# Expert weights split piecewise during attention and kept in DRAM, routing in two halves of the graphs, stage memory laid out anew: a graph attention layer followed by a mixture of experts on one core

## What is computed

```python
def gnn(x, adj, Wq, Wk, Wv, bv, Wo, bo):              # x is layernormed first
    q, k, v = x @ Wq.T, x @ Wk.T, x @ Wv.T + bv       # split into 12 heads of 32
    a = einsum('bnhd,bmhd->bhnm', q, k) * 384 ** -0.5 + adj[:, None]
    a = softmax(where(all(a == 0, -1), -inf, a))      # a row of zeros gives zeros
    return einsum('bhnm,bmhd->bnhd', a, v) @ Wo.T + bo

def moe(x, router_w, router_b, w1, b1, w2, b2, ln_g, ln_b):   # x is layernormed first
    logits = x.mean(axis=1) @ router_w.T + router_b   # one choice for each graph
    top_v, top_i = top_k(logits, 2); gates = softmax(top_v)
    h = act[e](x @ w1[e] + b1[e])                     # act: gelu, silu, mish, gelu
    y = sum(gate[e] * (h @ w2[e] + b2[e])) + x        # w1: 384x768, w2: 768x384
    return layernorm(y) * ln_g + ln_b

x = x + gnn(layernorm(x), adj, ...)
x = x + moe(layernorm(x), ...)
```

## Time and profile before

| | |
|---|---|
| median of 3 runs | 1682.14 us (1681.82 to 1683.52) |
| profiled execution | 1679.88 us, span 1678.1 us |
| TensorE busy | 1598.1 us, 95% of the span |
| VectorE, ScalarE, GpSimd busy | 1191.3, 953.4 and 826.9 us (71%, 57% and 49%) |
| TensorE's share of the chain that ended last | 88% |
| mean granted TensorE clock | 0.982 |
| DMA | 159.32 MB, 95 GB/s over the span |

### The profile page before, as it was taken

How to read it: one execution, slowest core, us unless ns; L and a number is a source line. 1 busy time by engine, 2 the same in 40 slices (tenths; PEclk the granted TensorE clock), 3 DMA queues, 4 the chain that set the end, 5 groups by cost and what they waited for, 6 DMA issues and landing times.

```text
span 1678.1 us, 44889 instructions
## 1 busy us (share of the span) xinstructions
PE 1598.1 (95%) x12732; PEld 1531.1 (91%) x12733; DVE 1191.3 (71%) x3613; ACT 953.4 (57%) x2780; POOL 826.9 (49%) x1239
## 2 busy tenths in 40 slices
PE   6999999999999999837999999999999999999997
PEld 6899999999999999727999999999999999999997
DVE  4788888888888887776666665666776766567764
ACT  4888888888888888744332332332433423243332
POOL 2777777777777777760233333323333233323333
PEclk9999999999999999958999999999999999999999
DMA  7233333333333332550122222222222222221221
GB/s 242 67 116 114 120 121 121 116 116 121 121 121 121 121 119 97 178 216 20 62 72 70 70 70 70 70 70 70 70 70 70 70 70 70 70 70 62 79 64 36
DMA packets 81260, 159.32 MB, mean 95 GB/s; under 512 B 8672, under 2 KB 46560, under 8 KB 80992
## 3 DMA queue, kind: packets, MB, share of 16 engines
q1 hardware_dynamic: 81120, 157.58, 27.6%
HBM read 94.64 MB, written 62.91 MB: 94 GB/s over the span
## 4 chain that ended last, share of the span: by engine, by line
PE 88%; DVE 5%; ACT 2%; issue 2%; SPq 1%; POOL 1%; DMA 1%; DVEq 0%; POOLq 0%; ACTq 0%
PE bank L368 68%; PE bank L437 5%; PE bank L526 5%; PE bank L396 3%; PE bank L460 3%; PE bank L477 2%; PE bank L469 1%; PE bank L446 1%; DMA x_in<-in_x 1%; DVE half_t L1027 1%; DVE inverse L1034 1%; DVE inverse L1030 1%; ACT at_hi L688 1%; ACT inverse L721 1%; ACT prob L599 1%
## 5 line engine op out<-in xcount | busy, mean ns | idle before, releaser
L368 PE MATMUL bank<-w_hi,ut_in 128*128 x1536 | 423.2, 343 | 32.3 <-issue 27.9
L599 ACT ACTIVATE prob<-att,neg_max 128x128 f32<-128x128 f32 x768 | 297.4, 391 | 34.4 <-DVE neg_max L871 34.3
L368 PEld LDWEIGHTS bank<-w_hi,ut_in 128*128 128x128 f32 x1536 | 280.8, 189 | 37.0 <-issue 37.0
L987 DVE SCALAR_TENSOR_TENSOR at_lo<-bank,gate_col,at_hi 128x384 fp32r<-128x384 f32 x256 | 146.1, 613 | 185.2 <-ACT at_hi L688 185.2
L368 PE MATMUL bank<-w_hi,at_hi 128*128 x768 | 258.0, 336 | 5.6 <-DVE at_lo L987 5.6
L368 PE MATMUL bank<-w_lo,ut_in 128*128 x768 | 257.9, 336 | 0.0
L368 PE MATMUL bank<-w_hi,at_lo 128*128 x768 | 257.1, 335 | 0.0
L368 PE MATMUL bank<-w_lo,at_hi 128*128 x768 | 256.7, 334 | 0.0
L688 ACT ACTIVATE at_hi<-bank,gate_col 128x384 fp32r<-128x384 f32 x256 | 134.5, 576 | 202.9 <-PE bank L526 201.0
L845 POOL TENSOR_SCALAR rs_z<-mv_z 128x1 f32<-128x1 f32 x64 | 14.7, 229 | 473.8 <-DVE mv_z L1053 473.8
L712 ACT ACTIVATE hid<-hid 128x384 f32<-128x384 f32 x192 | 95.1, 527 | 268.9 <-DVE hid L999 268.9
(11 more groups left out here) (136 smaller groups left out, 3820.9 us busy)
## 6 DMA issues: line engine op xcount, KB each, us to landing
xu_scratch<-xu SPq DMA_DIRECT2D x64, 384.0 KB, 2.3
ut_scratch<-ut_out SPq DMA_DIRECT2D x64, 384.0 KB, 2.7
ut_in<-ut_scratch SPq DMA_DIRECT2D x64, 384.0 KB, 2.9
xz<-xu_scratch SPq DMA_DIRECT2D x64, 384.0 KB, 3.0
x_in<-in_x SPq DMA_DIRECT2D x32, 384.0 KB, 4.4
xu<-in_x SPq DMA_DIRECT2D x32, 384.0 KB, 3.5
out_dram<-xz SPq DMA_DIRECT2D x64, 192.0 KB, 1.9
w_lo<-in_L_ffn_w SPq DMA_DIRECT2D x8, 1152.0 KB, 9.8
```

What stands on the lines that cost most here:

```text
L368: last = nc.tensor.matmul(acc, lhs[c][a], rhs[c][b], start=start and n == 0, stop=stop and n == len(terms) - 1)
L599: nc.scalar.activation(prob[g][:, hh, :], att[g][:, head, :], ACT.Exp, bias=neg_max[g][:, head:head + 1], scale=-1.0, accum_out=row_sum[g] ...
L987: nc.vector.scalar_tensor_tensor(out=flat(at_lo[:, s * DC:(s + 1) * DC, :]), in0=at_ps[s][:, 0:HALF], scalar=gate_col[:, col, 1:2], in1=fl ...
```

## The change

The expert weights are split during attention, in 48 pieces of 128x384, one at each step from 4 to 51. ScalarE rounds the piece into one of three staging tiles, VectorE subtracts, SP stores. For w1 the `lo` half stays where it was loaded and only the `hi` half goes to DRAM; for w2 the raw piece is loaded into a staging tile, and both halves go to DRAM. At the end of attention SP loads the halves back (`load_early`, steps 54 and 62 to 66), each as soon as the attention tiles under it are free; so do b1, b2 and the first two expert inputs. The stage memory is laid out so that these addresses come free in this order. Routing is done for 32 graphs at a time: the first half in steps 36 to 44 of attention, the second inside the expert steps of graphs 0 and 1. The gates come from tanh instead of exp and a division. ScalarE and VectorE wait at the start of the expert stage for the stores of attention, as SP did; the layernorm weights and the third and fourth `xz` are loaded when the second half of routing is done.

The new engine parts, cut to their core:

```diff
+    ROUTED = B // 2
+    PIECES = E * FC          # 24
+    FIRST = 4
+    w1h_dram = nc.dram_tensor("w1h_scratch", (E, P, DC, F), F32, kind="Internal").ap()
+    w2_dram = nc.dram_tensor("w2_scratch", (2, E, P, FC, D), F32, kind="Internal").ap()
...
+        def piece(h):
+            return h - FIRST if 0 <= h - FIRST < 2 * PIECES else None
+        def piece_tiles(j):
+            if j < PIECES:
+                e, c, s = j // FC, j % FC // 2, j % 2
+                return w1_lo[:, e, c, s * HALF:(s + 1) * HALF], stage_hi[j % 3][:]
+            return stage_lo[j % 3][:], stage_hi[j % 3][:]
...
# SP
-                if h == B - 1:
-                    sp.wait_ge(s_mm, B)
-                    for e in range(E - 1):
-                        load_w2(e)
-                    sp.wait_ge(exp_done, HEADS * (B - 1))
-                    sp.wait_ge(fold_done, FOLDS * (B - 1))
-                    load_w2(E - 1)
+            def store_piece(j):
+                sp.wait_ge(piece_lo, j + 1)
+                if j < PIECES:
+                    e, c, s = j // FC, j % FC // 2, j % 2
+                    sp.dma_start(w1h_dram[e, :, c, s * HALF:(s + 1) * HALF], stage_hi[j % 3][:].bitcast(F32)).then_inc(hi_stored[j % 3], 16)
+                else:
+                    e, c = (j - PIECES) // FC, (j - PIECES) % FC
+                    sp.dma_start(w2_dram[1, e, :, c], stage_hi[j % 3][:].bitcast(F32)).then_inc(hi_stored[j % 3], 16)
+                    sp.dma_start(w2_dram[0, e, :, c], stage_lo[j % 3][:].bitcast(F32)).then_inc(lo_stored[j % 3], 16)
+            def load_early(h):
+                if h == FIRST + 2 * PIECES + 2:
+                    for p in range(3):
+                        sp.wait_ge(hi_stored[p], 16 * (2 * PIECES // 3))
+                        sp.wait_ge(lo_stored[p], 16 * (PIECES // 3))
+                    load_w1_hi(0)
+                if h == B - 2:
+                    sp.wait_ge(qk_mm, 2 * B)
+                    load_w1_hi(1)
+                    load_w1_hi(2)
+                    sp.wait_ge(v_mm, B)
+                    load_w1_hi(3)
+                    sp.dma_start(b1_wide[:]...).then_inc(wide_loaded, 16)
+                    sp.wait_ge(xn_done, B)
+                    sp.dma_start(b2_wide[:]...).then_inc(wide_loaded, 16)
+                    sp.wait_ge(xt_mm, B)
+                    sp.wait_ge(ut_stored[0], 16)
+                    load_ut(0, 0)
+                if h == B - 1:
+                    sp.wait_ge(s_mm, B)
+                    load_w2(0, 0)
+                    sp.wait_ge(exp_done, HEADS * (B - 1))
+                    sp.wait_ge(fold_done, FOLDS * (B - 1))
+                    load_w2(0, 1)
+                if h == B:
+                    sp.wait_ge(exp_done, HEADS * B)
+                    sp.wait_ge(fold_done, FOLDS * B)
+                    load_w2(0, 2)
+                if h == B + 1:
+                    sp.wait_ge(pt_mm, PTC * B)
+                    load_w2(0, 3)
+                    sp.wait_ge(o_mm, B)
+                    load_w2(1, 0)
+                    sp.wait_ge(ot_done, B)
+                    load_w2(1, 1)
+                    sp.wait_ge(v_done, B)
+                    sp.wait_ge(xbo_done, B)
+                    sp.wait_ge(ut_stored[1], 16)
+                    load_ut(1, 1)
+                if h == B + 2:
+                    sp.wait_ge(wo_mm, B)
+                    load_w2(1, 2)
+                    load_w2(1, 3)
             for h in STEPS:
...
+                if piece(h - 1) is not None:
+                    store_piece(piece(h - 1))
+                if piece(h + 1) is not None and piece(h + 1) >= PIECES:
+                    load_piece(piece(h + 1))
+                load_early(h)
                 n = h - 3
                 if has(n):
                     reached(sp, u_done, n + 1)
# TensorE
+            def logits(half):
+                graphs = slice(half * ROUTED, (half + 1) * ROUTED)
+                pe.wait_ge(pooled_done, (half + 1) * ROUTED)
+                pe.wait_ge(const_ready, 2)
+                reached(pe, routed, half)
+                for e in range(E):
+                    for c in range(DC):
+                        last = nc.tensor.matmul(bank[7][:, D + e * ROUTED:D + (e + 1) * ROUTED], rw_wide[:, c, e, :], pooled[:, graphs, c],
+                                                start=c == 0, stop=c == DC - 1)
+                last.then_inc(logit_mm, 1)
             for h in STEPS:
...
+                if h == ROUTED + 4:
+                    logits(0)
                 if has(h - 1):
                     attend(h - 1)
...
+            logits(1)
             pe.wait_ge(routed, 1)
+            pe.wait_ge(w1h_loaded, 16 * E)
+            pe.wait_ge(piece_lo, PIECES)
...
+                            pe.wait_ge(w2_loaded, 32 * E)   # before the first second_layer
# ScalarE
+                reached(act, hi_stored[j % 3], 16 * (j // 3))
+                nc.scalar.activation(rounded, raw_piece.bitcast(F32), ACT.Copy).then_inc(piece_hi, 1)
...
+                nc.scalar.activation(g_tmp[:, 1, :], g_tmp[:, 0, :], ACT.Tanh, scale=0.5).then_inc(tanh_gap, 1)
             for h in STEPS:
                 if has(h - 2):
                     round_o(h - 2)
+                if h == B:
+                    nc.scalar.preload_act_table(ACT.Gelu)
                 if has(h + 4):
                     round_x(h + 4)
+                if piece(h) is not None:
+                    round_piece(piece(h))
+                if h == ROUTED + 10:
+                    tanh_of_gap(0)
                 if has(h):
                     exps(h, (0, 1))
...
             act.wait_ge(routed, 1)
+            for g in range(2):
+                for p in range(2):
+                    act.wait_ge(xu_stored[p][g], 16 * (B // 4))
+                act.wait_ge(ut_stored[g], 16 * (B // 2))
# VectorE
                 if has(h - 3):
                     sum_nodes(h - 3)
+                if piece(h) is not None:
+                    rest_of_piece(piece(h))      # wait piece_hi; lo = raw - rounded
                 if has(h - 1):
                     divide(h - 1)
                 if has(h + 2):
                     take_v(h + 2)
                 if has(h):
                     greatest_part(h)
+                if h == ROUTED + 5:
+                    route_choice(0, 0)           # 9 chained instructions on [P, 32, 4] or [P, 32]
+                if h == ROUTED + 7:
+                    route_choice(0, 1)           # 7
+                if h == ROUTED + 12:
+                    route_gates(0)               # 6; the fourth waits for the tanh
+            dve.wait_ge(routed, 1)
+            for g in range(2):
+                for p in range(2):
+                    dve.wait_ge(xu_stored[p][g], 16 * (B // 4))
...
             def expert_step(b, m, lap):
...
                     if graph(b, 0):
                         activate_second(b, k, e)
+                    if isinstance(b, int) and b == 0:
+                        route_choice(1, k)
+                    if isinstance(b, int) and b == 1 and k == 0:
+                        route_gates(1)
```

More of the change, by code:

```diff
@@ L87, in gnn_moe_kernel @@
         bv_wide = sb("bv_wide", [P, D], F32, s1)
+        bo_wide = sb("bo_wide", [P, D], F32, s1)
+        q_t = [sb(f"q_t{p}", [P, DC, 2 * N], F32, s1) for p in range(2)]
+        k_t = [sb(f"k_t{p}", [P, DC, 2 * N], F32, s1) for p in range(2)]
         raw = ExitStack()
@@ L119, in gnn_moe_kernel @@
         shift2 = [sb(f"shift2{g}", [P, 1], F32, s1) for g in range(2)]
-        sb("gap", [P, 640], F32, s1)
+        adj_in = [sb(f"adj_in{p}", [P, 2, N], F32, s1) for p in range(2)]
+        sb("gap", [P, 1024], F32, s1)
         rw_t = sb("rw_t", [P, DC, E], F32, s1)
@@ new lines, in load_w1_hi, with load_w2, load_ut @@
+            def load_w1_hi(e):
+                sp.dma_start(w1_hi[:, e].bitcast(F32), w1h_dram[e]).then_inc(w1h_loaded, 16)
+            def load_w2(half, e):
+                sp.dma_start((w2_lo, w2_hi)[half][:, e].bitcast(F32), w2_dram[half, e]).then_inc(w2_loaded, 16)
+            def load_ut(b, m):
+                source = ut_dram[b] if isinstance(b, int) else ut_dram[bass.ds(b, 1)].rearrange("o p s c n -> (o p) s c n")
+                sp.dma_start(ut_in[m % 2][:].bitcast(F32), source).then_inc(ut_loaded[m % 2], 16)
@@ L503, in _ @@
                     transpose_x(h + 5)
-            pe.wait_ge(pooled_done, B)
-            pe.wait_ge(const_ready, 2)
-            for e in range(E):
-                for c in range(DC):
-                    last = nc.tensor.matmul(bank[4][:, e * B:(e + 1) * B], rw_wide[:, c, e, :], pooled[:, :, c],
-                                            start=c == 0, stop=c == DC - 1)
-            last.then_inc(logit_mm, 1)
-            pe.wait_ge(routed, 1)
+            logits(1)
+            pe.wait_ge(routed, 1)
+            pe.wait_ge(w1h_loaded, 16 * E)
+            pe.wait_ge(piece_lo, PIECES)
+            pe.wait_ge(pt_act, 2 * B)
+            pe.wait_ge(pt_vec, B)
+            pe.wait_ge(ot_done, B)
```

(23 more changed lines are left out.)

185 lines of the change are left out of this document (77 added, 108 removed).

## The result

The changed kernel takes **1690.68 us** (median of 5 runs, 1689.87 to 1694.05) against 1682.14 for the kernel before. The ratio is 1.0056, 95% interval 1.0045 to 1.0066: slower by about half a per cent. The prediction was 1674.2, with 0.82 on faster, and 1690.7 lies outside its range of 1661 to 1682. The profiled execution took 1692.06 us, with a span of 1690.3.

A forecast was written before the change was run, and what follows sets the result against it. TensorE was taken to bound steady attention and the experts, leaving about 33 us at the hand-over. Hand-over and tail -14.0 plus attention +6.1 gave -7.9 us: 1674.2 against the median 1682.14, range 1661 to 1682.

The forecast's parts named there:

- about 33 us lie open to this change; all else can only lose: Hand-over from attention to experts, 728.38 to 761.74 us: the only stretch where the change was held able to gain.
- rival A: The forecast itself: the DMA queue ends the hand-over; range 1669 to 1679 us, chance 0.60.
- D: Hand-over: the store wait grows until the expert stage starts as late as before; no change, 1682 us, chance 0.10.
- C: Attention: the pieces lengthen the steady step, up to 0.5 us each, 1698 us; chance 0.15 for some such cost.
- 48 pieces at 0: Steady attention: weight-split pieces, one a step, fit existing waits and slack and cost 0 us; upper bound 24.
- logits(0) at +2.6: Attention: the first half's logits, 12 fp32 products in 24 records, add 2.6 us on TensorE; bounds 1.3 and 5.1.
- Routing in attention at 3.5: VectorE's two choices and gates for the first half add 2.0, 1.3 and 0.2 us; bounds 0 and 8.1.
- The tail: End of attention: residual load queued behind 6.29 MB lands 5.9 us late, less 0.72 of wait, delaying everything after by 5.2.
- The queue ends the hand-over: Hand-over: attention's last stores, queued behind weights, land about 748 us and decide; second hidden block gains 16.0 before attention's 6.1.
- Choice 1 at 2.0: Early experts: the second half's choice 1 on VectorE, ahead of a block taken with no wait, loses 2.0 us.
- The second gates at 0: Early experts: the second half's gates, 1.4 us, are covered by TensorE's second layer and cost 0.
- Hand-over and tail together: From attention's tail into the first expert graphs: 16.0 us gained less 2.0 for choice 1, so -14.0.

The follow-up runs named there:

- e1: Changed kernel plus 60 filler instructions (long fulfilled waits) on VectorE ahead of the expert loop, moving only the loop's place; 1676.83 us, ratio 0.9971.
- e2: Kernel before plus 68 filler instructions on VectorE, so its loop starts where the changed kernel has it; 1699.94 us, ratio 1.0108.
- e4: Changed kernel with SP's early loads of a step moved behind that step's stores, residual load and adj load; 1691.79 us, ratio 1.0058.
- e6: e1 with three of eight w2 loads (3.5 MB) issued behind the first two xz loads, not ahead of attention's last two stores; 1669.0 us.
- e9: e6 with the second choice of the second half of routing moved into VectorE's wait for at_hi; 1667.45 us, ratio 0.9913.
- e5: e1 with routing of the second half moved right behind VectorE's last attention step, ahead of its waits for the stores; 1675.99 us, ratio 0.9967.
- e7: The changes of e5 and e6 together, filler included; 1675.69 us, ratio 0.9970 against the kernel before.
- e10: e9 with e4's order on SP, early loads behind the step's stores, residual load and adj load; 1670.74 us, ratio 0.9931.
- e12: Changed kernel plus 100 filler instructions on VectorE ahead of the expert loop; 1676.26 us in its one run.
- e3: Changed kernel plus 128 filler instructions on VectorE ahead of the expert loop, one whole fetch block; 1690.2 us, ratio 1.0052.
- e11: Changed kernel plus 30 filler instructions on VectorE ahead of the expert loop; 1688.55 us in its one run.

## Why the prediction was wrong

**The step that failed** is a term put at nothing without a reason: "about 33 us lie open to this change; all else can only lose", and then no cost at all for the 916 us of the experts. The stage lost 15.9 us through VectorE's waits at the back edge (3.07 to 3.46 us, with five fetches each), and e1 and e2 show that the loop's place alone turns the sign. With the loop in a fast place the changed kernel has 1676.83. That is 2.6 us from the 1674.2 of the forecast and inside the range of rival A (1669 to 1679). Against the kernel before beside it that is 4.9 us gained, where 7.9 were forecast. None of rivals A to D held the mechanism. D had named a loss at the hand-over, C one in attention, which was 0.

**48 pieces at 0:** right. TensorE's first scores of graphs 0 to 36 start a constant 0.55 us later than before, which is no cost of the pieces, since other runs with the same attention start between 0.5 us earlier (e4) and 1.2 us later (e1); the steady step is 10.70 us with pieces as without. Rival C is refuted.

**logits(0) at +2.6:** right. The step at graph 37 is 2.6. No trace shows a frequency for the clock levels that the prediction names; they show the shares 1.00 and 0.50, and only the ratio of these enters the sum.

**Routing in attention at 3.5:** a size. The three steps are 1.9, 1.55 and 0.9, 4.4 together. The 0.5 us in it for a wait behind GpSimd's `ot_lo` was an estimate from the earlier trace rows; no run isolates it. Attention became 7.0 us longer, not 6.1. The trace has two loads of an activation table, at 0.7 and 717.6 us, and none at the tanh of attention; the sum has no term for one either.

**The tail:** right in mechanism, a little small. The residual load was to land near 720, it was issued at 719.08 and used at 722.29, some 2 us later; GpSimd waited 6.3 us, where the load was worked out to be 5.9 late. The last pooled graph is begun at 741.31 instead of 727.83, 13.5 us later, where 6.1 + 5.2 = 11.3 were forecast.

**The queue ends the hand-over:** right, and e6 shows it: 3.5 MB less ahead of the last stores gave 7.8 us. The second hidden block came at 763.50 instead of about 762. That is 8.0 us gained where the forecast, with attention's 6.1, had 9.9.

**Choice 1 at 2.0:** 2.45 (e9), and a term that the sum lacked: the 2.7 us for which TensorE idles there are followed by 3.4 us at granted clock 0.50, in which 36 products take 8.08 us instead of 6.53.

**The second gates at 0:** right. VectorE is done with them early enough to wait another 0.78 us for TensorE.

**Hand-over and tail together:** the shift is -3.8 at graph 3, where the sum said -7.9. Of those 4.1 us the second hidden block misses 1.9, choice 1 another 0.5, and the clock behind it 1.6.

**The sum:** -7.9 forecast, -3.8 measured before the loop, +15.9 in the loop, +12.2 in the profiled spans (1690.3 against 1678.1; the parts are rounded), +8.5 in the medians. The two profiled executions lie apart from their medians, 2.3 below and 1.4 above.

## What to carry to other kernels

A hardware loop whose text doesn't change can still change its time, since instructions ahead of it move it against the fetch blocks: 60 of them, less than half a block of 8192 bytes, made 13.9 us here (1690.68 to 1676.83). Before a change is judged by its time, look at the packets of instruction fetch within the loop (65 against 1 here) and at "issue" behind its back edge (4.33 us at the jump shown, against 1.13 in e1). If they rise, move the loop by a fraction of a block with instructions that lie in idle time, and compare again.

What fills idle time must be put where the idle time is after the next edit as well: 60 instructions of fulfilled waits cost nothing in e1 and about 6 us in e5 and e7.

Loads that are wanted later should be issued behind the stores on which the next stage waits, as long as they still land before they are read: moving three of them gained 7.8 us in e6, though TensorE then waited 2.4 us for them, and 3.4 in e10, where they started later.

A loss shouldn't be put down to the instructions that stand where it arises: ahead of the fourth hidden block stood the second gates, and what had grown was the time of TensorE's 36 products at granted clock 0.50 (8.08 us against 6.53).

## What the runs showed of the hardware

A loop of 324 instructions on VectorE jumped back 13 times with one fetch or none on queue 14 (before, e1, e12), or with five blocks of 8192 bytes each time (65 or 66; changed kernel, e2, e3, e11), by its place alone. At 12 of the 13 back edges the sequencer then went on after 2.75 to 3.46 us instead of 0.32 to 0.36.

Fulfilled waits weren't free: 60 instructions, of two such waits each, took 5.9 us on VectorE (754.84 to 760.74 in e5).

The logits' products with 32 columns gained nothing over 64: 24 of them took 5.33 us at the hand-over of e6 (granted clock 0.50), where the 24 of the earlier trace rows took 5.38. In attention, at granted clock 1.00, they cost the 2.6 us that the prediction took and not its lower bound of 1.3.

Granted clock behind idle time of TensorE: 2.7 us of idle time in the changed kernel (773.5 to 776.2) were followed by 0.50 from 777.5 to 780.9, and 2.9 us behind the ninth back edge (1331.9 to 1334.8) by 0.50 from 1333.8 to 1340.7. In e3 TensorE idled 3.1 us behind the same back edge and the clock stayed at 1.00, so the length of one idle time alone doesn't decide it.
